# State-space scan: the second feature tile's inflow made by TensorE from diagonals, its decay kept in SBUF, its read-outs done by GpSimd

## The reference, cut to what matters

```python
u = _silu(conv(x_in)); x_dbl = u @ x_proj.T          # splits into dt, Bm, Cm (16 numbers per token each)
delta = softplus(dt @ dt_proj.T + dt_proj_b)
A = -jnp.exp(A_log)
def step(h, inp):
    d_t, b_t, c_t, u_t = inp
    h = h * jnp.exp(d_t[:, :, None] * A) + (d_t * u_t)[:, :, None] * b_t[:, None, :]
    y = jnp.einsum('bdn,bn->bd', h, c_t)
    return (h, y)
y = ys + u * D_param
y = y * _silu(z)
```

## Time and profile before

| | |
|---|---|
| median of 3 runs | 2816.51 us (2804.28 to 2836.14) |
| the profiled execution, time | 2810.85 us |
| its span, first to last instruction | 2809.1 us |
| mean granted clock of TensorE | 0.908 |
| TensorE, VectorE, ScalarE, GpSimd busy, whole span | 85%, 65%, 48%, 19% |
| the phase of the scan | from 1930.2 us to some 2190 us of the span |
| in it (1925 to 2190): VectorE, GpSimd, TensorE, ScalarE busy | 250.24, 216.93, 147.48, 83.47 of 265 us |

### The profile page before, as it was taken

The page is one execution under the profiler, slowest core; times in us unless marked ns, Lnnn a source line. Parts: engine busy times, 40 slices in busy tenths (PEclk is TensorE's granted clock), DMA queues, the critical chain, the costliest instruction groups (busy, mean ns, idle before and its releaser), DMA issues. The chain is left out here.

```text
span 2809.1 us, 37743 instructions
## 1 busy us (share of the span) xinstructions
PE 2389.3 (85%) x12764; PEld 1015.2 (36%) x12764; DVE 1820.9 (65%) x4357; ACT 1355.8 (48%) x2317; POOL 525.9 (19%) x618
## 2 busy tenths in 40 slices
PE   6799999999999999999779798994556996999848
PEld 4333334333433433333244423441122432433225
DVE  3686767777776777777227765356999334877442
ACT  3365666665666666566526123425333421566610
POOL 1210111110111111010014101005798001100010
PEclk7799999999999999999979898987899995999968
DMA  2231222222122212222010000003243003222020
GB/s 92 79 93 42 84 66 70 67 78 63 61 79 79 70 55 78 63 64 65 17 40 1 22 1 27 1 10 101 106 149 127 30 9 93 81 69 66 29 103 16
DMA packets 77450, 171.59 MB, mean 61 GB/s; under 512 B 23049, under 2 KB 38665, under 8 KB 73163
## 3 DMA queue, kind: packets, MB, share of 16 engines
q1 hardware_dynamic: 77258, 169.18, 19.0%
HBM read 128.41 MB, written 39.71 MB: 60 GB/s over the span
## 5 line engine op out<-in xcount | busy, mean ns | idle before, releaser
L1056 ACT ACTIVATE sb_prob<-ps 128x512 f32<-128x512 f32 (+1 forms) x1520 | 805.7, 575 | 482.8 <-PE ps L846 307.6
L820 PE MATMUL ps<-sb_k_stack_half,sb_q_stack_half 78*128 78x512 bf16 (+3 forms) x1920 | 588.0, 340 | 55.0 <-DMA sb_q_stack_half<-q_rows 23.7
L846 PE MATMUL ps<-sb_q_stack_half,sb_k_stack_half 81*128 81x128 bf16 (+2 forms) x2240 | 570.3, 312 | 53.6 <-ACT sb_prob L1056 51.9
L957 DVE TENSOR_REDUCE sb_row_max<-ps 128x1 f32<-128x512 f32 x640 | 432.3, 687 | 139.9 <-PE ps L820 138.0
L966 DVE CUSTOM_DVE_ANT_0 sb_masked_scores<-ps,sb_mask_row,sb_row_max 128x128 bf16<-128x128 f32 (+3 forms) x640 | 341.5, 544 | 92.8 <-PE ps L820 89.6
L966 DVE CUSTOM_DVE_ANT_0 sb_masked_scores<-ps,sb_mask_row 128x128 bf16<-128x128 f32 (+3 forms) x640 | 283.3, 488 | 172.9 <-PE ps L820 172.1
L846 PEld LDWEIGHTS ps<-sb_q_stack_half,sb_k_stack_half 81*128 81x128 bf16 x2240 | 201.8, 99 | 385.8 <-ACT sb_prob L1056 201.9
L867 PE MATMUL ps<-sb_prob,sb_v_first_half 128*9 128x512 f32 (+3 forms) x2560 | 299.5, 541 | 0.2 <-ACT sb_o_raw L1063 0.2
L820 PEld LDWEIGHTS ps<-sb_k_stack_half,sb_q_stack_half 78*128 78x128 bf16 x1920 | 184.5, 100 | 267.2 <-DVE sb_row_max L966 79.3
L2682 PE MATMUL ps<-sb_read_out,sb_ident 128*128 128x512 f32 x256 | 140.6, 681 | 118.5 <-DVE sb_read_out L2769 112.5
L2736 POOL TENSOR_TENSOR sb_inflow<-sb_delta_u,sb_b_spread 128x1024 f32<-128x1024 f32 x64 | 201.5, 3163 | 26.6 <-DVE sb_states L2758 19.0
(11 more groups left out here) (372 smaller groups left out, 3236.2 us busy)
## 6 DMA issues: line engine op xcount, KB each, us to landing
sb_q_stack_half<-q_rows SPq DMA_DIRECT2D x240, 96.0 KB
sb_k_stack_half<-k_rows SPq DMA_DIRECT2D x40, 576.0 KB
o_rows<-sb_o_raw SPq DMA_DIRECT2D x80, 256.0 KB, 2.3
sb_b_spread<-b_rows SPq DMA_DIRECT2D x32, 512.0 KB, 4.8
sb_c_spread<-c_rows SPq DMA_DIRECT2D x32, 512.0 KB, 3.5
sb_k_stack_half<-k_rows SPq DMA_DIRECT2D x40, 288.0 KB
q_rows<-sb_qk_parts SPq DMA_DIRECT2D x60, 128.0 KB, 2.1
k_rows<-sb_qk_parts SPq DMA_DIRECT2D x60, 128.0 KB, 2.1
```

Source lines behind the costliest of these rows:

```text
L820: pe.matmul(M.ps[:, k % RING, 0:hi - lo], qst[half][0:S1_ROWS, s, j, at:at + P], kst[half][0:S1_ROWS, s, lo // CH, j, 0:hi - lo], start=Tr ...
L846: mm = pe.matmul(bank[:, x * w + lo:x * w + hi], kst[half][0:S2_ROWS, s, t // 4, j, t % 4 * P:(t % 4 + 1) * P], qst[half][0:S2_ROWS, s, j, ...
L957: dve.reduce_max(rowmax[:, tau % 3, 0, at:at + 1], M.ps[:, k % RING, 0:w], AX_X).then_inc(first_done, 1)
L1056: act.activation(prob[:, st % PROB_STEPS, heads[0]:heads[-1] + 1, a:CH], scores.rearrange("p (j q) -> p j q", j=len(heads)), ACT.Exp).then ...
```

## The change

The two feature tiles of a group no longer go the same way.

- Tile 0 is as before, but with two buffers for the inflow in place of three, and one decay buffer in PSUM (two banks) in place of two.
- Tile 1's inflow is made by TensorE. Once per batch TensorE turns `delta_u` of tile 1 (eight 128-column matmuls with the identity, `turn`), and ScalarE copies it to `delta_u_by_token`. For each group ScalarE makes eight diagonal matrices, the identity scaled by a column of B (`diagonal`, eight ACTIVATEs of 128x128), and TensorE multiplies the two (`inflow`, eight matmuls of 128 columns) into two PSUM banks, of which there is one set. B by token is made once at the start with 16 small matmuls and one copy.
- Tile 1's decay goes to SBUF (the buffer of `h_T`, two halves), and its scan reads the decay from SBUF and the inflow from PSUM.
- Tile 1's read-out is made by GpSimd.
- States and read-outs have two buffers per tile. `b_spread` has two buffers, `c_spread` three.

The core of the diff, with the waits that the prediction speaks of:

```diff
@@ TensorE
+                    def inflow(g):
+                        b, n = groups[g]
+                        pe.wait_ge(turned_copied, b + 1)
+                        pe.wait_ge(diag_ready, g + 1)
+                        if g:
+                            pe.wait_ge(scanned1, g)
+                        for blk in range(QB):
+                            mm = pe.matmul(M.ps[:, INFLOW_BANK + blk // 4, blk % 4 * P:(blk % 4 + 1) * P],
+                                           duT[:, blk, :], diag[:, g % 2, blk, :], start=True, stop=True)
+                        mm.then_inc(inflow1_ready, 1)
+
+                    def gather(g, d):
+                        b, n = groups[g]
+                        pe.wait_ge(read[d], g + 1)
                         if n == 0 and b:
                             pe.wait_ge(y_ready, DI * (b - 1) + d + 1)
...
-                    for i in range(LAST):
-                        gather(i)
+                    for g in range(G):
+                        if g == NS:
+                            turn(1)
+                        inflow(g)
+                        if g:
+                            gather(g - 1, 0)
+                        if g >= 2:
+                            gather(g - 2, 1)
@@ ScalarE
+                    def diagonal(g):
+                        b, n = groups[g]
+                        if g >= 2:
+                            act.wait_ge(inflow1_ready, g - 1)
+                        for blk in range(QB):
+                            ins = act.activation(diag[:, g % 2, blk, :], M.ident[:], ACT.Copy,
+                                                 scale=btok[:, b * QB + blk, n:n + 1])
+                        ins.then_inc(diag_ready, 1)
...
+                        if g == NS - 1:
+                            take_turned(1)
+                        if g + 1 < G:
+                            diagonal(g + 1)
@@ GpSimd
+                    def read_out(g):
+                        pool.wait_ge(scanned1, g + 1)
+                        pool.wait_ge(c_in[g % BR[1]], 16 * (g // BR[1] + 1))
+                        if g >= 2:
+                            pool.wait_ge(summed1, g - 1)
+                        pool.tensor_tensor(hc[:, 1, g % 2, :], st[:, 1, g % 2, :], csb[:, g % BR[1], :],
+                                           ALU.mult).then_inc(read1, 1)
+
+                    for g in range(G):
+                        inflow(g)
+                        if g:
+                            read_out(g - 1)
@@ VectorE
+                    def scan1(g):
+                        dve.wait_ge(decay1_ready, g + 1)
+                        dve.wait_ge(inflow1_ready, g + 1)
+                        if g >= 2:
+                            dve.wait_ge(read1, g - 1)
+                        dve.tensor_tensor_scan(st[:, 1, g % 2, :], decay1[:, g % 2, :], two_banks(INFLOW_BANK), 0.0,
+                                               ALU.mult, ALU.add).then_inc(scanned1, 1)
...
+                    for g in range(G):
+                        scan0(g)
+                        if g:
+                            read_out(g - 1)
+                        if g == NS + 1:
+                            total(0)
+                        scan1(g)
+                        if g == 3:
+                            for d in range(DI):
+                                dve.wait_ge(exp_done, d + 1)
+                                dve.tensor_scalar(one[:, d, :], ex[:, d, :], 1.0, None, ALU.add).then_inc(plus, 1)
+                        elif g in (7, 8):
+                            d = g - 7
+                            dve.wait_ge(plus, d + 1)
+                            softplus_end(dve, done, d, 1, pre1, log_done, slope_ready, delta_ready)
```

More of the change, by code:

```diff
@@ L2644, in tb @@
                 return tmp.enter_context(sbuf(nc, name, shape, dt))
-            R, BR = 3, 3
-            dBu = tb("inflow", [P, R, T])
-            st = tb("states", [P, R, T])
-            hc = tb("read_out", [P, R, T])
-            bsb = tb("b_spread", [P, BR, T])
-            csb = tb("c_spread", [P, BR, T])
-            groups = [(b, n) for b in range(B) for n in range(NS)]
-            LAST = DI * len(groups)
-            HALF = DI * NS
-            with phase(nc, *[f"b_in{s}" for s in range(BR)], *[f"c_in{s}" for s in range(BR)], "decay_ready", "inflow_ready", "scanned", "read",
-                       "summed", "y_ready", "weighted0", "weighted1", "out_ready", "added", "abs_done", "exp_done",
-                       "plus", "slope_ready", "log_done", "chain", "delta_ready", "du_ready") as (block, *sems):
-                b_in, c_in = sems[:BR], sems[BR:2 * BR]
-                (decay_ready, inflow_ready, scanned, read, summed, y_ready, weighted0, weighted1, out_ready,
-                 added, abs_done, exp_done, plus, slope_ready, log_done, chain, delta_ready, du_ready) = sems[2 * BR:]
+            BR = (2, 3)
@@ new lines, in mamba @@
+            dBu = tb("inflow", [P, 2, T])
+            st = tb("states", [P, DI, 2, T])
+            hc = tb("read_out", [P, DI, 2, T])
+            bsb = tb("b_spread", [P, BR[0], T])
+            csb = tb("c_spread", [P, BR[1], T])
+            diag = tb("b_diagonal", [P, 2, QB, P])
+            duT = tb("delta_u_by_token", [P, QB, P])
+            btok = tb("b_by_token", [P, NBLK, NS])
+            decay1 = M.h[:].rearrange("p (s t) -> p s t", s=2)
+            groups = [(b, n) for b in range(B) for n in range(NS)]
@@ new lines, in mamba, with two_banks @@
+            G = len(groups)
+            DECAY_BANK, INFLOW_BANK, Y_BANK = 0, 2, 4
+            def two_banks(at):
+                return M.ps[:, at:at + 2, :].rearrange("p a t -> p (a t)")
+            with phase(nc, *[f"b_in{s}" for s in range(BR[0])], *[f"c_in{s}" for s in range(BR[1])], "btok_ready",
+                       "btok_copied", "turned", "turned_copied", "diag_ready", "decay0_ready", "decay1_ready",
+                       "inflow0_ready", "inflow1_ready", "scanned0", "scanned1", "read0", "read1", "summed0", "summed1",
+                       "y_ready", "weighted0", "weighted1", "out_ready", "abs_done", "exp_done", "plus",
+                       "slope_ready", "log_done", "chain", "delta_ready", "du_ready") as (block, *sems):
+                b_in, c_in = sems[:BR[0]], sems[BR[0]:sum(BR)]
+                (btok_ready, btok_copied, turned, turned_copied, diag_ready, decay0_ready, decay1_ready, inflow0_ready,
+                 inflow1_ready, scanned0, scanned1, read0, read1, summed0, summed1, y_ready, weighted0, weighted1,
+                 out_ready, abs_done, exp_done, plus, slope_ready, log_done, chain, delta_ready,
+                 du_ready) = sems[sum(BR):]
+                read, summed = (read0, read1), (summed0, summed1)
@@ new lines, in read_out @@
+                    def read_out(g):
[9 more added lines that the diff above has]
+                            read_out(g - 1)
+                        if g in (9, 10):
+                            e = g - 9
@@ L2747, in _ @@
                                                ALU.mult).then_inc(weighted0, 1)
+                    read_out(G - 1)
                 @block.vector
@@ L2778, in _ @@
-                    for i in range(LAST + 1):
-                        if i < LAST:
-                            scan(i)
-                        if i:
-                            read_out(i - 1)
-                        if i in (7, 8):
-                            d = i - 7
-                            dve.wait_ge(exp_done, d + 1)
-                            dve.tensor_scalar(one[:, d, :], ex[:, d, :], 1.0, None, ALU.add).then_inc(plus, 1)
-                        elif i in (14, 15):
-                            d = i - 14
+                                                     two_banks(Y_BANK + 2 * d), ALU.mult, ALU.add).then_inc(y_ready, 1)
@@ L2789, in _ @@
                             dve.wait_ge(plus, d + 1)
                             softplus_end(dve, done, d, 1, pre1, log_done, slope_ready, delta_ready)
-                        elif i == HALF + 2:
-                            total(0)
+                    read_out(G - 1)
                     total(1)
```

165 lines of the change are left out of this document (97 added, 68 removed).

## The result

Four timed runs of each kernel on one chip: 2813.9 us before (2804.28 to 2836.14) and 2839.0 after (2836.37 to 2844.98). The ratio is 1.0106, 95% interval 1.0072 to 1.0139 (the quotient of the two medians is 1.0089). The forecast was 2846, 1.07% up. A second set of runs on another occasion gave 1.0091 (1.0064 to 1.0118).

The account below looks back on a forecast made before the run. VectorE and GpSimd take turns at a shared port; after the change a loop through TensorE's gathers gives 7.24 us per group, was 6.63. Terms sum to +30 on span 2809.1, time 2841, median 2846; 8-in-10 range 2812 to 2872.

Follow-up runs that it names:

- e4: The changed kernel with tile 1's read-out given back to VectorE, behind its scan of tile 1; phase 293.2 us against the changed kernel's 277.0.
- e8: e4 with a third buffer for B's rows; phase 293.7 us.
- e7: The changed kernel with each group's eight inflow matmuls on TensorE issued twice, same result; undisturbed groups 7.37 us, phase 282.3 us against 277.0.
- e2: The changed kernel with TensorE's gather(g-2, 1) ahead of gather(g-1, 0); 2800.8 us median of 10 runs, ratio to before 0.9974, phase 248.2 us.
- e10: e4 with B's load of the next group issued ahead of C's load; undisturbed groups 6.63 us, phase 256.6 us.

## What to carry to other kernels

Two engines that share a port have to be placed in time, not only counted. Ask of each use which event releases it and whether that event lies just ahead of the other engine's request; if both hang on one circle, the collision repeats in each round, as it did here in after and again in e4 and e8. The cure need not be less work: a swap of two steps on a third engine was worth 1.66 us of an undisturbed group's 7.37 here, and a swap of two loads 2 of 8.6.

When a loop gets faster, price again the other work in it, both what its slack had hidden and which of its operations now meet the other engine at the port: here nearly half of the loop's gain went back into these.

## What was not expected of the hardware

- TensorE's last gather to GpSimd's start took 0.18 us (also 2133.72 to 2133.90 in e7), where VectorE's read-out to TensorE's gather takes 0.06 and tile 1's scan to GpSimd's read-out 0.08 (2117.57 to 2117.65 in e2).
- In a loop in which TensorE is busy 48.75 of 60 us, the granted clock falls for single pairs of gathers (5.40 for 3.70), at the same groups in two profiled executions.
- e7, with 5.3 us more phase, had a shorter span than after (2827.9 against 2835.1), with 621.4 us behind the phase in place of 637.0. The other kernels have 625.1 to 635.8 there. It is a single execution of each, and whether the doubled matmuls caused it stays open.
- VectorE's adding one (TENSOR_SCALAR, one input) took 2.83 and 2.85 us in before, and 0.66 and 0.68 in after, where GpSimd was waiting for TensorE: so it loses the port too, though it reads only one tile.
- The wait for a load that a profile lists (150 us of GpSimd in e4) cost nothing in itself: in e10 GpSimd still idles 114 us in front of the same products. What cost was the moment at which the wait ended.
